# Unread TensorE products in the routing stage of an attention and mixture-of-experts layer

## The reference, cut to what matters

```python
logits = einsum('th,eh->te', h, router_weight)
probs = softmax(logits)
topk_probs, selected = top_k(probs, 2)
topk_probs = topk_probs / max(topk_probs.sum(-1), EPS)
# each expert takes up to 1280 tokens; a token's place in its expert is a running count
dispatch = where(slot < capacity, expert * capacity + slot, FC)
expert_inputs[dispatch] = h[token]
pre  = einsum('ech,edh->ecd', expert_inputs, ff_pre_act_weight)
gate = einsum('ech,edh->ecd', expert_inputs, gate_weight)
expert_out = einsum('ecd,ehd->ech', pre * silu(gate), ff_post_act_weight)
out[token] += expert_out[dispatch] * kept_weight
```

## Time and profile before

| what | value |
|---|---|
| median of three runs | 1740.58 us (1739.08 to 1740.96) |
| profiled execution | 1734.3 us |
| its span | 1732.5 us |
| PE busy | 1623.6 us, 94% of the span |
| ACT busy | 1255.3 us, 72% |
| DVE busy | 1141.7 us, 66% |
| POOL busy | 299.1 us, 17% |
| mean granted TensorE clock | 0.977 |

### The profile page before, as it was taken

One profiled execution on the slowest core, in us unless ns is written; L12 is line 12 of the kernel. 1 busy time (PEld: TensorE's weight loads), 2 busy tenths in 40 slices (PEclk: granted clock), 3 DMA queues, 4 the chain that ended last, 5 costly groups with the idle time before them and its releaser, 6 DMA issues. The chain is left out here.

```text
span 1732.5 us, 31337 instructions
## 1 busy us (share of the span) xinstructions
PE 1623.6 (94%) x12878; PEld 952.0 (55%) x12878; DVE 1141.7 (66%) x1766; ACT 1255.3 (72%) x1350; POOL 299.1 (17%) x247
## 2 busy tenths in 40 slices
PE   8979999999999999999999984699999999999995
PEld 6723333333333333333333333589998988889985
DVE  7847687777776878777868777445354444644475
ACT  7869999999999999999999976333343333433333
POOL 1000000000000000000310000424243515425144
PEclk9979999999999999999999997899999999999998
DMA  7691030300300303003021002213142313324043
GB/s 255 217 258 60 1 88 1 76 13 2 88 1 1 88 1 77 11 2 88 1 98 50 1 26 98 96 39 107 15 112 62 73 55 70 84 44 109 8 134 121
DMA packets 78897, 118.29 MB, mean 68 GB/s; under 512 B 9202, under 2 KB 62811, under 8 KB 78734
## 3 DMA queue, kind: packets, MB, share of 16 engines
q1 hardware_dynamic: 63840, 98.32, 19.1%
q0 software_dynamic: 14880, 17.82, 5.8%
q10 hardware_dynamic: 32, 0.07, 0.0%
HBM read 80.22 MB, written 40.37 MB: 70 GB/s over the span
## 5 line engine op out<-in xcount | busy, mean ns | idle before, releaser
L918 DVE TENSOR_REDUCE sums<-expq 128x1 f32<-128x1536 f32 (+7 forms) x576 | 559.6, 1034 | 175.7 <-ACT expq L891 175.3
L891 ACT ACTIVATE probs<-scores 128x1536 f32<-128x1536 f32 (+1 forms) x384 | 509.2, 1478 | 11.7 <-PE scores L796 11.5
L891 ACT ACTIVATE expq<-scores 128x1536 f32<-128x1536 f32 x320 | 447.4, 1536 | 2.5 <-PE scores L796 0.9
L818 PE MATMUL o_ps<-probs,v 128*32 128x256 f32 (+1 forms) x4864 | 348.0, 368 | 0.0
L796 PE MATMUL scores<-aq,ak 98*128 98x512 bf16 (+3 forms) x1280 | 304.8, 353 | 11.0 <-PEq L620 9.5
L1576 ACT ACTIVATE gate<-up_ps 128x512 f32<-128x512 f32 x128 | 76.6, 599 | 326.0 <-PE up_ps L1400 315.6
L796 PE MATMUL scores<-ak,aq 98*128 98x512 bf16 (+3 forms) x1184 | 265.1, 343 | 22.7 <-ACT probs L891 16.9
L796 PEld LDWEIGHTS scores<-aq,ak 98*128 98x128 bf16 x1280 | 95.1, 98 | 215.5 <-ACT expq L891 75.5
L1400 PE MATMUL up_ps<-xeT_hi,wup_hi 128*128 128x512 f32 x512 | 203.1, 397 | 4.5 <-issue 2.5
L1888 DVE TENSOR_TENSOR mid<-up_ps,gate 128x512 f32<-128x512 f32 x128 | 88.4, 691 | 177.0 <-ACT gate L1576 167.8
L1400 PE MATMUL up_ps<-xeT_lo,wup_hi 128*128 128x512 f32 x512 | 202.2, 395 | 0.0
(11 more groups left out here) (261 smaller groups left out, 1906.8 us busy)
## 6 DMA issues: line engine op xcount, KB each, us to landing
raw<-w_T SPq DMA_DIRECT2D x16, 1024.0 KB
split_dram<-parts SPq DMA_DIRECT2D x48, 256.0 KB, 3.0
aq<-split_dram SPq DMA_DIRECT2D x42, 256.0 KB
ak<-split_dram SPq DMA_DIRECT2D x42, 256.0 KB
raw<-wg_T SPq DMA_DIRECT2D x8, 1024.0 KB
v_dram<-vst SPq DMA_DIRECT2D x8, 544.0 KB, 4.6
v<-v_dram SPq DMA_DIRECT2D x8, 544.0 KB, 10.8
xT<-x_T SPq DMA_DIRECT2D x8, 512.0 KB, 6.0
```

The source lines that it names most:

```text
L818: last = nc.tensor.matmul(o_ps[g % O_RING][32 * h:32 * h + 32, col:col + w], value(gg, k, h, 32), probs[:, m % 2 * GH + h, at:at + w], sta ...
L891: nc.scalar.activation(dst, src[:, 0:w], ACT.Exp, scale=HD ** -0.5).then_inc(exp_done, 1)
L918: last = nc.vector.tensor_reduce(sums[:, gg % 2, col, h:h + 1], expq[:, at % X_RING, lo:lo + w], AX.X, ALU.add)
```

## The change

Three groups of products whose result nobody reads are put into TensorE's list: 12 behind the last turning of the logits, after a new wait for `logit_off` (VectorE's last subtraction before the exponential); 14 behind the prefix products; 18 behind the lists and the branch, just ahead of the wait for the first gathered rows. Each multiplies `ident` (as weights) with `after` (128 x 512, plain f32) into `up_ps[1][:, 1, :]`, which nothing holds at that time. The waits that stood there stay, behind the products.

```diff
+UNREAD = (12, 14, 18)
...
                 by_token(1)
+                def unread(n):
+                    for _ in range(n):
+                        nc.tensor.matmul(up_ps[1][:, 1, :], ident[:], after[:].rearrange("p r k -> p (r k)"), start=True, stop=True)
+
+                pe.wait_ge(logit_off, 1)
+                unread(UNREAD[0])
                 pe.wait_ge(keep_ready, 1)
                 prefix_products(ALL).then_inc(prefix_ready, 1)
+                unread(UNREAD[1])
                 for n in range(NP):
                     list_piece(n, 0)
...
+                unread(UNREAD[2])
                 pe.wait_ge(xin_loaded[0], 16 * NA)
                 turn(0, 0)
```

## The result

The changed kernel takes 1741.71 us against 1738.97 in the same series of 20 runs each: a ratio of 1.0018 (95% interval 1.0013 to 1.0024), or about 3.1 us more.

The account below looks back on a forecast made before the run. TensorE's work bounds the kernel up to the first expert, with its clock falling to half in idle waits. Terms 0.0 + 5.6 - 0.8 - 2.1 = +2.7 us took the median from 1740.58 to 1743.3; 8-in-10 range 1739.8 to 1746.5.

Parts of the forecast that it names:

- The copy 2.2 us late: First group, 12 products, delays the prefix products; VectorE's copy gets them at 1062.45 instead of 1060.19.
- PEclk 1.0 from 1040 on throughout: Sign in the profile: TensorE's granted clock stays full from 1040 us on.
- Won back by the first piece: First list piece takes 2.4 instead of 4.62 us, recovering the 2.2 us lost in the picks.
- The turning 5.6 us late: Third group, 18 products, ends at 1113.0; the turning of rows now starts at 1107.42: +5.6 us.
- The branch: TensorE's flag load and untaken branch before the third group: 0.8 us taken, ends 0 and 1.4.
- The price of a product: Time of one unread plain f32 product at the full clock: 0.88 us, ends 0.86 and 0.92.
- 0.8 us back between turning and up product: From the turning's start to the first up product, 2.6 instead of 3.38 us at the full clock: -0.8.
- 2.1 us back in the up products: First 48 up products take 10.99 instead of 13.06 us at the full clock: -2.1.
- delay swallowed: Rival: ScalarE's remote wait in the first expert ends at a fixed time, swallowing up to 0.9; +1.8, 1742.4; chance 0.09.
- the end of the lists: Shift where the list pieces end: 0.0; -0.2 at 0.86 us a product, +0.6 at 0.92.
- the low end, +1.3: Lower end of the summed change: 0.86 us a product and no branch cost, about +1.3 us.
- about -6: Filling that ends in time: -1.0 in the prefixes, -2.2 in the first piece, -2.9 in the third group.

Follow-up runs that it names:

- the third chip: Last group of runs, four kernels on one chip; the kernel before takes 1735.60 us, the changed kernel 1738.59, ratio 1.0016.
- the second chip: Second group of runs, on another chip, where the kernel before takes 1731.06 us.
- late gather: GpSimd gathers the next expert's rows only after six ScalarE gates of the current one; changed kernel with it on the second chip 1733.93 us, 1.0015 of before.
- the first pair of profiles: The kernel before and the changed kernel as profiled ahead of the follow-ups: 78.76 and 84.73 us from `keep` to the first down product.
- the second alone: Only the 14 products behind the prefix products, the other two groups left out, against the kernel before: 1734.20 us, ratio 0.9989.
- fitted kernels: Kernels whose product counts should let each group end before or just as its operand comes; ratios to the kernel before 0.9967 to 0.9991.
- the kernel before with the late gather: No unread products, only GpSimd's gather delayed until six ScalarE gates, against the kernel before on the second chip: 1732.80 us, ratio 1.0007.
- 10, 14, 13, 1: Product counts, first ten not waiting for `logit_off`, one after the turning; against before: 0.9970 with late gather, 0.9967 without (the second chip), 0.9991 (the third chip).
- 8, 14 and 12: The three groups cut to 8, 14 and 12 products, against the kernel before: 1732.50 us, ratio 0.9981.
- the first group alone: Only the first 12 products, the other two groups left out, against the kernel before: 1739.63 us, ratio 1.0022.
- the one of +22 us: Changed kernel with the late gather, run again on the third chip, against the kernel before: 1756.96 us, ratio 1.0127.
- the first chip: First group of runs, where the kernel before takes 1736.27 us; it ran the groups one by one and the counts 8, 14, 12.

## Why the prediction was right, step by step

The two profiles of the third chip serve best, since both have the hold and neither a dip. Their `keep` to first down product differs by 82.13 - 79.46 = 2.67 us; the runs by 2.8. (The spans of these two executions differ by -2.1 us, since the picks were ready 2.5 us sooner in the second, so a span by itself says little here.)

- *The copy 2.2 us late*: 1.98, because a product costs 0.86 and not 0.88. In the first profile it was 3.7, for the dip of the clock. That dip, 1.7 us, was missing in the sum, and the sign "PEclk 1.0 from 1040 on throughout" failed there. I had read the clock as 1.0 up to 1053 and called it kept; the group started after TensorE had idled 1.10 us, and 0.72 before that. Where the group waited for `logit_off`, the clock fell in four of six profiles. With the first ten products put at the end of the turning at once, it stayed at 1.0 in all three.
- *Won back by the first piece*: right, -0.20 at the third `in_q` against before.
- *The turning 5.6 us late*: 4.39. The branch costs nothing, where I took 0.8, and 18 products take 15.45 and not 15.84. The price of a product and the branch were both at the low end of their ranges.
- *0.8 us back between turning and up product*: 0.79.
- *2.1 us back in the up products*: 0.72 here, -0.84 (a loss) in the first profile. This term left a wait out. The up products do run at the full clock, but where there is a hold, the first expert can't pass the gate that ScalarE holds until 28.5 to 30.2 us after `slot_row`. I had seen this wait, and priced it at up to 0.9 us of delay swallowed. It rather swallows the gain: a TensorE that is further on waits longer. The term was also too large by itself. In the pair of the second chip with the late gather, which has no hold, 1.33 come back (24.32 against 22.99), since the first 48 up products took 12.60 us there before and 11.28 after, where the earlier trace rows gave 13.06 and 10.99:

```profile
1112.26 12.60 PE up_ps L1401 x48
```

```profile
1117.24 11.28 PE up_ps L1409 x48
```

The sum came out right because two terms were too dear, by 1.2 in the turning and 0.2 at the end of the lists, and one gain was too large, by 1.4. That these cancel is luck. By the measured prices alone my sum would have been the low end, +1.3.

There is a second piece of luck. The sum takes everything behind the first expert as unchanged, and the part on it above shows that it was not. Counted from `keep` to TensorE's last product, the changed kernel is 4.8 us longer in the first pair of profiles, 3.0 in the pair with the late gather and 0.3 in the pair of the third chip. The +2.7 lies among these, but single profiles can't bear it out to the tenth. What they do bear out, each time, are the delays: the copy by 2.0 or 3.7 us, the turning by 4.3 to 4.4.

One more step, used for "about -6" with fitted counts, was wrong: the prefix products have no microsecond to give. With the products on time the copy starts 2.09 us behind `keep` against 2.24, since VectorE itself weighs the picks until then. The 0.18 us that the copy waited for TensorE in the earlier trace rows said so beforehand. The first group can gain only by starting the second at the full clock: 0.3 us at the third `in_q` (17.23 with the second alone, 16.93 with both). The gain of the fitted kernels is the first piece's 2.3 us and, where there is no hold, some 1 us in the third stretch: 36.67 in the kernel before with the late gather against 35.52 and 35.91. With the hold that stretch gives nothing. On the second chip the kernel before with the late gather takes 6.5 and 7.3 us more than the two fitted ones. The table has 2.7 and 2.3 of these (there the kernel before won 0.8 at the first piece by a clock that rose sooner), and 2.5 and 3.6 lie behind the first down product.

The trace agrees with the clock rule of the Trainium skill (TensorE: Matmul & The Clock Gate, Why this matters for your kernels), which asks for no idle gaps between bursts of products, as far as it goes: in the three profiles with 10, 14, 13, 1 products the granted clock is 1.00 from 1040 to 1230. That the filling has to fit is shown by the two kernels on one chip: 12, 14, 18 against 10, 14, 13, 1 costs 4.9 us on the third and 7.7 on the second, as the table has it.

Two things remain open. One is what holds ScalarE. With the gather moved the hold was absent on the third chip (one profile against three), but on the second it was absent in one profile with the gather in place too, so the gather is not the whole cause, and that it is part of it rests on a single profile. No experiment named the mechanism. The other is what the length of the list does, as said above.

## What to carry to other kernels

Price a filler instruction by its records before counting it out, and let the group end before its operand can come: an overrun delays what stands behind it, and the clock gives back only what the next stretch had cost at the low clock. Ask of each gain what else ends just there; here VectorE's own work stood right behind one such stretch and ScalarE's hold behind another. Start the filling at the end of the last real work, not at a later signal. And when a change adds instructions, compare the far end of the kernel as well: a gap may have moved there that has nothing to do with the idea.

## What the runs showed of the hardware

- The granted clock can fall during products that follow 1 to 2 us of gaps, though they run back to back: 0.50 in 1053 to 1055 of the changed kernel. It did in three of four profiles of the changed kernel (two of them with the late gather) and in that with 8, 14 and 12, not in that with the first group alone.
- The first rows land 9.9 to 10.3 us behind `slot_row` in the fitted kernels, 8.9 to 9.1 where TensorE is idle. Whether the filling causes it was not tried.
- A gap of 0.6 to 1.6 us in TensorE's issue stood at the same distance behind the first down product in all profiles of one kernel, on different chips (but for the one of +22 us), and elsewhere when the number of unread products was another. Its cause is not shown.
- One gate of ScalarE was held until 28.5 to 30.2 us after `slot_row` in all profiles of the first chip and three of four of the third, in none of the second; and one kernel that is 1.0015 of before on one chip and 1.0127 on another.
